# Attention and routing of a mixture-of-experts block on one core: V as the stationary operand, reciprocals turned instead of results, experts marked by match_replace

## The reference, cut to what matters

```python
x = x + xattn(layernorm(x), ctx, Wq, Wk, Wv, Wo, bo)
#   qp, kp, vp = q @ Wq.T, kv @ Wk.T, kv @ Wv.T   (kv has 192 features), 4 heads of 64
#   attn = softmax(qh @ kh.T * 64**-0.5);  ctx = attn @ vh;  return ctx @ Wo.T + bo
x = x + ffn(layernorm(x), ...)
#   scores = softmax(xf @ gw + gb)                          32 experts in 8 groups of 4
#   group score = sum of its two best; keep the 4 best groups
#   indices = the 4 best experts in the kept groups; weights = their scores
#   y = sum over experts of weight * ((silu(x@w1+b1) * (x@w3+b3)) @ w2 + b2)
#   z = (silu(x@sw1+sb1) * (x@sw3+sb3)) @ sw2 + sb2         the shared expert; returns y + z
```

## Time and profile before

| | before |
|---|---|
| median of 3 runs | 395.49 us (395.03 to 395.94) |
| the profiled execution | 394.26 us |
| its span, first to last instruction | 392.5 us |
| TensorE busy | 332.1 us, 85% |
| VectorE busy | 268.4 us, 68% |
| ScalarE busy | 184.0 us, 47% |
| GpSimd busy | 167.7 us, 43% |

### The profile page before, as it was taken

How to read it: one execution, slowest core, us unless ns; L and a number is a source line. 1 busy time by engine, 2 the same in 40 slices (tenths; PEclk the granted TensorE clock), 3 DMA queues, 4 the chain that set the end, 5 groups by cost and what they waited for, 6 DMA issues and landing times.

```text
span 392.5 us, 9872 instructions
## 1 busy us (share of the span) xinstructions
PE 332.1 (85%) x2356; PEld 284.5 (72%) x2357; DVE 268.4 (68%) x910; ACT 184.0 (47%) x622; POOL 167.7 (43%) x202
## 2 busy tenths in 40 slices
PE   3999999999999989997999999989898989895000
PEld 2698888888898968785876988778787878684000
DVE  4588597877878696989574565665675645664585
ACT  2486675757567564345112654544545545443000
POOL 4703005352536263556241255555565454555300
PEclk9999999999999999999699999999999999999555
DMA  6897718475612721202314455455555554554898
GB/s 162 287 384 285 241 27 298 149 251 170 210 67 103 290 103 48 88 33 100 115 67 128 118 170 165 150 175 169 155 164 162 163 170 139 176 163 170 328 385 296
DMA packets 33766, 68.96 MB, mean 176 GB/s; under 512 B 5323, under 2 KB 26092, under 8 KB 32076
## 3 DMA queue, kind: packets, MB, share of 16 engines
q1 hardware_dynamic: 26348, 46.95, 37.3%
q0 software_dynamic: 6960, 21.11, 14.7%
q10 hardware_dynamic: 432, 0.59, 0.6%
HBM read 39.87 MB, written 28.77 MB: 175 GB/s over the span
## 4 chain that ended last, share of the span: by engine, by line
PE 41%; DVE 17%; issue 15%; DMA 9%; SPq 7%; ACT 5%; another core or an unknown queue 1%; ACTq 1%; POOL 1%; DVEq 1%; POOLq 0%
PE psS L1166 6%; PE psF L961 5%; DMA xn2T_all<-dispatch 4%; PE psS L1155 4%; PE psS L93 3%; DVE nmax L1232 3%; PE psF L1175 3%; SPq L483 3%; PE psF L1166 3%; SPq L123 2%; DMA w<-shares 2%; PE psF L93 2%; PE psG L1000 2%; PE psS L940 2%; PE psF L1065 1%
## 5 line engine op out<-in xcount | busy, mean ns | idle before, releaser
L657 POOL DMA_INDIRECT shares<-xn2T_all,e_number x81 | 81.1, 1001 | 77.5 <-PE psF L1175 43.3
L614 POOL DMA_INDIRECT dispatch<-work,slot_now x64 | 62.6, 978 | 96.9 <-issue 45.4
L1166 PE MATMUL psS<-work,arena 128*128 128x128 f32 x432 | 57.1, 275 | 0.0
L1166 PEld LDWEIGHTS psS<-work,arena 128*128 128x128 f32 x432 | 52.6, 192 | 0.1
L861 ACT ACTIVATE work<-psS 128x256 f32<-128x256 f32 x81 | 30.9, 383 | 34.9 <-PE psS L1155 20.4
L1626 DVE SCALAR_TENSOR_TENSOR work<-psS,b,work 128x128 f32<-128x128 f32 x54 | 18.8, 349 | 38.8 <-ACT work L872 30.4
L1155 PE MATMUL psS<-ident,xn2T_all 128*128 128x128 f32 x162 | 32.0, 280 | 9.0 <-issue 6.6
L1155 PEld LDWEIGHTS psS<-ident,xn2T_all 128*128 128x128 f32 x162 | 20.6, 141 | 23.5 <-issue 12.5
L1629 DVE COPY arena<-w 128x512 f32 x81 | 35.9, 444 | 2.0 <-issue 2.0
L1175 PE MATMUL psF<-w,work 128*128 x108 | 32.9, 387 | 2.7 <-issue 2.5
L872 ACT ACTIVATE work<-psS,b 128x128 f32<-128x128 f32 x54 | 19.9, 368 | 30.3 <-PE psS L1166 22.0
(11 more groups left out here) (227 smaller groups left out, 794.9 us busy)
## 6 DMA issues: line engine op xcount, KB each, us to landing
xn2T_all<-dispatch SPq DMA_DIRECT2D x81, 160.0 KB
w<-in_w SPq DMA_DIRECT2D x6, 1536.0 KB
w<-shares SPq DMA_DIRECT2D x6, 1024.0 KB, 7.0
dispatch<-padding SPq DMA_DIRECT2D x8, 640.0 KB
w<-in_w SPq DMA_DIRECT2D x1, 2304.0 KB
x<-in_x SPq DMA_DIRECT2D x1, 1536.0 KB, 7.2
w<-shares SPq DMA_DIRECT2D x3, 512.0 KB, 10.9
out<-x SPq DMA_DIRECT2D x3, 512.0 KB, 3.7
```

The costliest lines, as they stand in the source:

```text
L614: pool.indirect_dma_start(dispatch, bass.IndirectOffsetOnAxis(ap=slot_now[:, par, j * TOPK + k:j * TOPK + k + 1], axis=0), xn2[:, par, j, ...
L657: pool.indirect_dma_start(shares, bass.IndirectOffsetOnAxis(ap=e_number[:, u:u + 1], axis=0), e_y[:, u, :], None).then_inc(added[u], 16)
L1166: ins = pe.matmul(hidden_bank(u)[:, m * P:(m + 1) * P], e_w13k[:, u % UNROLL, k, m * INTER:(m + 1) * INTER], e_xT[:, u % 3, k, :], start=( ...
```

## The change

On **TensorE** `attend(b)` is one call behind both `probs_T`. V is stationary (64 columns) and 256 turned probabilities move; the result is already turned, and two heads lie in the two halves of the partitions. `attend_T` is gone. In its place `shares_T` turns the reciprocal sums, which **GpSimd** has widened to 64 equal columns per head (`widen`), **ScalarE** copies them (`turned_out`), and **VectorE** divides in one operation of 128 by 512 (`divide`). `ranks` ends with a transposition of the marks (`chosenT`), and `rank_index` makes the numbers of the shares from that behind `probs_T(b,1)`. The **routing** uses pair sums of the exponentials, `max` and `match_replace` on the group sums and on the masked experts, and a comparison with the mark; the weights are divided by the sum only at the end. The rows for dispatch are found by `max`. There are 14 counted constants instead of 17, and TensorE waits for all of them at the start where it waited for 13. GpSimd's loop is written out. SyncE's load of late expert weights waits for `turned_psum` too. The **order** changes on every engine.

```diff
@@ TensorE, scores, then shares_T and attend
+                if not isinstance(b, int) or b >= 1:
+                    pe.wait_ge(s["pT_ready"], TPB * (b - 1) + (j + 1))
...
-            def attend(b, j, par, front):
-                pe.wait_ge(s["pT_ready"], TPB * b + (j + 1))
...
-                for hp in range(HEADS):
-                    h = (hp % 2) * 2 + hp // 2
-                    for t in range(2):
-                        ins = pe.matmul(psF[:, 2 - j, h * HD:(h + 1) * HD], pT[:, j, t, hp, :], v_sb[:, par, t, h * HD:(h + 1) * HD],
+            def shares_T(b, front):
+                pe.wait_ge(s["wide_ready"], b + 1)
...
+                        ins = pe.transpose(shares_bank(b)[:, k * LQ + j * P:k * LQ + (j + 1) * P],
+                                           wide[:, j, k].rearrange("p r d -> p (r d)"), ident[:, :])
+            def attend(b, par, front):
+                pe.wait_ge(s["pT_ready"], TPB * (b + 1))
...
+                for k in range(KD):
+                    y = psF[:, 1, k * LQ:(k + 1) * LQ].rearrange("p (j q) -> p j q", j=TPB)
                     for t in range(2):
+                        for r in range(2):
+                            h, rows = 2 * k + r, slice(r * HD, (r + 1) * HD)
+                            ins = pe.matmul(y[rows], v_sb[:, par, t, h * HD:(h + 1) * HD], pT[:, :, t, 2 * r + k, :],
+                                            start=(t == 0), stop=(t == 1))
@@ shared stage on TensorE
                 if c == 0:
                     ranks(last - 1)
+                    rank_index(last - 1)
+                if c == 3:
+                    rank_index(last)
@@ GpSimd
+            def widen(b):
+                pool.wait_ge(s["prcp_ready"], b + 1)
...
+                for j in range(TPB):
+                    ins = pool.tensor_copy(wide[:, j], spread(prcp[:, j, :].rearrange("p (r k) -> p k r", k=KD), 3, HD))
+            for b in range(2, BATCHES):
+                widen(b)
+                scatter(b - 2, b % 2, (("attT_psum", b + 1), ("scores_psum", TPB * (b + 2)) if b + 1 < BATCHES else ("sh_psum", KS * 2), ("proj_psum", TPB * b + 2)))
@@ VectorE
+            def divide(b):
+                dve.wait_ge(s["turned_ready"], b + 1)
+                dve.wait_ge(s["attT_psum"], b + 1)
+                dve.tensor_tensor(attT, psF[:, 1, :].rearrange("p (k q) -> p k q", k=KD), turned, ALU.mult)
...
+                    ins = dve.match_replace(marked[:, j, :], top[:, j, 0:8], masked[:, j, :], MARK)
```

More of the change, by code:

```diff
@@ new lines, in scatter @@
+            def scatter(b, par, paced):
+                wait_apart(pool, s["slots_ready"], b + 1)
+                if b >= 1:
+                    pool.wait_ge(scattered, 16 * TPB * TOPK * b)
+                scatter_pair(b, par, 0)
+                for pair, (event, nth) in enumerate(paced, 1):
+                    wait_apart(pool, s[event], nth)
+                    scatter_pair(b, par, pair)
+                pool.tensor_copy(cw[:, TPB * b:TPB * b + TPB, 0:EXPERTS], xn2[:, par, :, D:D + EXPERTS]).then_inc(s["cw_kept"], 1)
@@ L740, in round_context, with step @@
                 act.activation(ctx_high[0:KC, par], ctx_now[0:KC, par], ACT.Copy).then_inc(s["ctx_rounded"], 1)
-            def step(b, par, front, front2, tail, nth=None):
+            def step(b, par, front, front2, tail, tail2, nth=None):
+                first = isinstance(b, int) and b == 0
                 if front:
@@ L838, in _ @@
                     norm2_out(last)
+                if c == 3:
+                    chosen_out(last)
                 if c + 2 < BATCHES:
@@ L846, in _ @@
                         norm2_keep(last)
+                if c == 0:
+                    chosen_out(last - 1)
                 if c in (1, 2):
@@ L1071, in step @@
                     proj_k(b + 1, 1 - par)
+                probs_T(b, 0)
                 if front:
                     proj_v(b + 1, 1 - par)
-                probs_T(b, 0)
-                if not front:
+                else:
                     pe.wait_ge(s["x1_ready"], TPB * (b - 1) + 1)
                     shared_up(0, 0)
-                if tail2 and front:
+                if tail2:
                     ranks(b - 2)
                 probs_T(b, 1)
-                if not front:
-                    pe.wait_ge(s["pT_ready"], TPB * b + 1)
-                    shared_up(0, 1)
-                    ranks(b - 2)
-                if tail:
-                    norm2_T(b - 1, 1 - par)
-                attend(b, 0, par, front)
-                if tail:
-                    gate(b - 1)
-                attend(b, 1, par, front)
+                if tail2:
+                    rank_index(b - 2)
                 if front:
@@ L1093, in step @@
                 else:
-                    shared_up(1, 0)
-                attend_T(b, front)
+                    pe.wait_ge(s["pT_ready"], TPB * b + 1)
+                    shared_up(0, 1)
+                if front2:
+                    norm_T(b + 2)
+                shares_T(b, front)
+                attend(b, par, front)
+                if tail:
+                    norm2_T(b - 1, 1 - par)
                 if front:
@@ L1098, in step @@
                 else:
+                    shared_up(1, 0)
                     shared_up(1, 1)
-                if front2:
-                    norm_T(b + 2)
-                project(b)
+                if tail:
+                    gate(b - 1)
+                project(b, front)
             pe.wait_ge(s["wk_in"], 16)
             proj_k(0, 0)
-            pe.wait_ge(s["consts"], CONSTS - 4)
+            pe.wait_ge(s["consts"], CONSTS)
             norm_T(0)
@@ L1363, in rank_rows, with route_weights @@
+            def route_weights(b, par):
+                dve.wait_ge(s["chosen_ready"], b + 1)
+                for j in range(TPB):
+                    dve.scalar_tensor_tensor(xn2[:, par, j, D:D + EXPERTS], masked[:, j, 0:EXPERTS], grcp[:, j:j + 1], chosen[:, j, :], ALU.mult, ALU.mult)
             def rank_rows(b):
```

477 lines of the change are left out of this document (217 added, 260 removed).

## The result

The change made the kernel slower: 403.66 us (median of four runs, 401.65 to 405.48) against 395.3 of the kernel before, ratio 1.0208, 95% interval 1.0158 to 1.0258. Forecast were 387.0 us and a range from 382.5 to 395.5. On two other chips, where both kernels are faster, the same two kernels stand the other way round: 369.13 against 376.95 us (0.9845, 0.9754 to 0.9937) and 372.97 against 375.78 (0.9908, 0.9869 to 0.9948). The prediction was wrong for the comparison it was made for, and that the sign depends on where the two are run is half of what follows.

The account below looks back on a forecast made before the run. TensorE was taken to bound the attention steps, VectorE second. Terms -11.8 - 1.7 + 2.1 + 0.6 + 2.2 = -8.6 us took the profiled 394.26 to 385.7; the median lying 1.2 above gave 387.0 us, range 382.5 to 395.5.

Parts of the forecast that it names:

- Steps 1 to 6: Attention steps: TensorE saves 1.7 us in the first and 2.35 in each of the other five, 11.8 in those.
- Rival 1: Attend's column halves don't run together: 0.215 us an instruction, +1.3 in each of eight steps, 397.2 us, slower; 15%.
- the estimate ahead: Attend: each of 16 instructions also pays a 53 ns weight load, 4.3 us; about 404 us; not in the sum.
- match_replace: Routing on VectorE: not in the trace, priced like FIND_INDEX8 with its load, 0.18 and 0.08 us; twice that as other end.
- Step 7: Last attention step: TensorE waits over 4 us for VectorE's residual, 21.1 us instead of 19.05, +2.1; shared stage's head +0.6.
- Step 0: First attention step: the wait for norm_T(2), now ahead of attend, takes what the products give: 0, within 1 us.
- Clock: TensorE's clock behind the full stop of 4 us: two thirds of a 3.3 us loss, +2.2, bounds 0 and 3.3.
- rival 2: A new wait in the steps, 1 us in each of five or more: 392 us (389 to 396); 17%.
- exps(b+1,1) is now queued behind gate_exps: ScalarE's order in the steps: it ends near 2 us into the next step and is asked for near 6.
- The expert stage should be the same to 1 us: Expert stage behind the shared stage: code is kept, so its time should be the same to 1 us.

Follow-up runs that it names:

- c2: Group of runs on one more chip: the kernel before, the changed kernel and two variants; the kernel before took 376.21 us, the changed kernel 372.97.
- c2_before: The kernel before, unedited, run on one more chip: 376.21 us.
- c2_after: The changed kernel, unedited, run on the same chip as c2_before: 372.97 us, 0.9908 of the kernel before.
- f2_step0: The changed kernel with norm_T(2) in step 0 put back behind the attention product and second score product: 366.22 us, 0.9715 of the kernel before.
- c1_after: The changed kernel, unedited, as control on another chip: 369.13 us, 0.9845 of the kernel before.
- e1: The changed kernel with the last two scatters of a batch moved past the next widening, in five batches: 418.56 us, 1.0536 of the kernel before.
- e4: The changed kernel with e1's edit, chosen_out ahead of norm on ScalarE, and nearly the old order in the last step: 416.16 us, 1.0511 of the kernel before.
- e5: The changed kernel with unused products filling TensorE's idle places in steps 0 and 7 and ahead of shared_down(0): 364.62 us, 0.9685 of the kernel before.

## Why the prediction was wrong, step by step

Two steps failed. The clock was priced at +2.2 us, with 3.3 as its bound, and cost 9.6 on the first chip and 7.9 on that of c2; and ScalarE's q_out, with the signal it waits for, was given no price at all. The chip without held signals measures the forecast's own terms; the figures of the list are from c2_before and c2_after.

- **Steps 1 to 6: right.** Forecast -1.7 and five times -2.35, in all -13.5 us; measured -1.5, -2.3, -2.4, -2.2, -2.2 and -2.1, in all -12.7. A step takes 15.6 us (forecast 15.9), VectorE 12.4 (11.5), attend 1.88 (2.1).
- **Rival 1 (column halves): fell**, at 0.117 us an instruction. The Trainium skill, "TensorE: Matmul & The Clock Gate", section on LDWEIGHTS, would have given 4.3 us by the estimate ahead; the trace doesn't agree: the 16 take 1.88 us with their loads.
- **match_replace** is recorded at 0.16 and 0.18 us with a load of 0.09: as its row.
- **Step 7: right in size.** Forecast 21.1 us and a wait of over 4 on VectorE's residual; measured 21.5 us from probs_T(7,0) to shared_down(0) (130.08 to 151.61), 2.6 more than the 19.0 of c2_before, the wait 4.56.
- **Step 0: wrong.** "The wait takes what the products give: 0, within 1 us." Step 0 takes 17.6 us for 15.7, +1.9: the wait is 2.3 and the clock behind it loses 1.7 more, less the 2.1 that the other changes save there (step 0 takes 13.6 in f2_step0, without wait and low clock). What failed is that I took the wait to be no longer than the gain, and priced no low clock behind it. The trace also starts step 0 later by 0.7, which is within what the start differs between runs (18.0 to 19.8).
- **Clock: mis-sized.** Forecast +2.2, bounds 0 and 3.3, as two thirds of one stretch like the earlier trace rows. Measured 9.6 us lost against 1.7, +7.9: one stretch of 13.7 us (6.2 lost) behind the full stop, where I had taken 6.5, and one of 3.4 in step 0 (1.7); the one later has its like in the kernel before. Behind the same stop of 4.6 us the low clock lasted 10.2 us in two traces (the changed kernel's first, f2_step0) and 13.7 in two (c1_after, c2_after). A length seen once is no bound.
- Sum on that chip: -12.7 + 2.6 (the start and step 0) + 8.1 (step 7 and the shared stage, clock in it) - 1.1 (the rest) = -3.1 us, where -8.6 was forecast. The clock alone, 7.9 for 2.2, is more than the difference.

**On the first chip more was added, and a part of it was rival 2's kind, at a place I hadn't seen.** By the same parts the sum there is -8.1 (steps 1 to 6), +2.1, +13.6 and +3.7: against the other chip 4.6 us more in the steps, 5.5 in step 7 and the shared stage, 4.8 in the experts' stage and 0.5 less at the start. "A new wait in the steps" had 17% and 389 to 396 us, and I sought it in GpSimd's copies. It was ScalarE's q_out, which wasn't among the moved work's prices: "exps(b+1,1) is now queued behind gate_exps", I wrote, and looked only at whether they came late. What the new order took away was their cover: ScalarE was now free for q_out 1.9 us after the product of q began, in the stretch in which signals are held. The profile before had the sign, q_out with 1.0 us of "remote" and a silu with 4.8, which I passed over as somebody else's. With the waits that follow from it, it costs some 1.7 us in each of steps 3 to 5 (17.3 against 15.6), where the kernel before loses 0.2 to 0.5 (18.5, 18.4 and 18.0 against 18.0, 17.9 and 17.8). At the head of step 7 the late residual costs a wait of 2.3 us, with 4.5 us lost to the clock from there on.

**"The expert stage should be the same to 1 us": right** on the chip of c2, within rounding (163.2 and 162.1); on the first it took 3.7 us more in the one profile, with the same code. Why is open: ScalarE's waits for TensorE's products in that stage are up to 3.1 us long there and at most 1.5 in c2_after, and the changed kernel's four runs spread over 3.8 us where the kernel before spreads over 0.9.

## What to carry to other kernels

When a tuned order is changed, price each new wait of TensorE twice: once as a wait, once as a stretch of idleness behind which all its work may run at half speed for 3 to 14 us. Here a better order of step 0 and the last step, with chosen_out's place, was worth more (9.9 us) than the whole rewrite on the same chip (7.8), and even useless products in the holes gained 4.5. And before work is taken out from in front of a wait, look what else it covered; a stall with no releaser in the profile is a stall like any other. Compare on more than one chip: the sign of this change turned between the first and the two others on which both kernels were timed.

## What the runs showed of the hardware

- On the chips of the first comparison and of e1 to e4, TensorE's semaphore updates came late, in the changed kernel by up to 3.7 us, in the later part of a run of GpSimd's indirect writes, and together when it ended; in steps without a scatter they took 0.01. On the chips of the other comparisons none was over 0.03 us late ahead of the experts' stage. There the two kernels took 369 to 377 us instead of 395 to 404, and the experts' stage 162 and 163 us instead of 180 and 177. Whether this is the chip, the recording (some 40% of the update records are missing in the traces with held signals) or something else that differed between the jobs isn't settled.
- The last pair of a scatter, issued right behind a weight load of 1.5 MB, was waited for 7.3 and 6.1 us, though its descriptors were on another queue; in the step without a load the wait was 1.6 us (e1).
- TensorE's granted clock fell to its lower level (1.2 GHz) for 3.4 us behind a wait of 2.3 us (c1_after, c2_after) and for 10.2 to 13.7 us behind one of 4.6 (f2_step0, c1_after, c2_after). With products that nobody uses in these places it stayed at the upper level (e5).
- Two f32 instructions with 64 stationary columns each and 256 moving ones run side by side, 0.117 us apiece, in either order of the halves.
